# A graph layer on one core: the TensorE fetch moves to three bf16 parts of its table and takes 24 chunks over five late chunks each, in place of 20 over seven

## The reference, cut to what matters

```python
xs = x[src]                                              # 200000 edges, x is 6250 x 64, float32
deg_w = max(seg(w), 1);  deg_c = max(seg(1), 1)          # seg sums over the edges with the same dst
gcn   = seg((w / sqrt(deg_w[src] * deg_w[dst]))[:, None] * xs) @ Wgcn + bgcn
sage  = x @ Wsage_s + seg(xs) / deg_c[:, None] @ Wsage_n + bsage
agg_w = seg(w[:, None] * xs)
gin   = ((1 + gin_eps) * x + agg_w) @ Wgin + bgin
gconv = x @ Wgc1 + agg_w @ Wgc2 + bgc
eop   = seg(w[:, None] * relu(xs + edge_attr)) @ Wedge + bedge
out   = layernorm(x + sum_k weights[k] * [gcn, sage, gin, gconv, eop][k])
```

## Time and profile before

| | us |
|---|---|
| median of three runs | 2227.15 (2219.24 to 2228.43) |
| the profiled execution's own time | 2228.75 |
| its span, first to last instruction | 2226.9 |
| first late product of the rounds, to the first of the plain step | 475.70 to 2166.97 |
| last late product starts | 2189.03 |
| indirect DMAs on POOL for late chunks | 1280 |
| mean granted TensorE clock | 0.867 |

### The profile page before, as it was taken

How to read it: one execution, slowest core, us unless ns; L and a number is a source line. 1 busy time by engine, 2 the same in 40 slices (tenths; PEclk the granted TensorE clock), 3 DMA queues, 4 the chain that set the end, 5 groups by cost and what they waited for, 6 DMA issues and landing times.

```text
span 2226.9 us, 22565 instructions
## 1 busy us (share of the span) xinstructions
PE 1556.4 (70%) x6037; PEld 1007.5 (45%) x6037; DVE 928.6 (42%) x2539; ACT 826.9 (37%) x1201; POOL 1355.2 (61%) x1426
## 2 busy tenths in 40 slices
PE   1004367566888777877878778777887888877876
PEld 1003367553554544544445445444444445544546
DVE  5684256543433332433433433243333334423346
ACT  1676233243433433424244234233333324423323
POOL 7665366556666656656666666566666656665660
PEclk9999967688989888978889888888888888888988
DMA  5111234331222222222222222222222222222223
GB/s 98 23 24 51 70 100 112 95 80 42 51 64 45 55 54 46 57 46 44 54 57 53 47 57 43 47 58 50 48 66 43 48 51 57 47 53 44 59 55 77
DMA packets 83186, 126.12 MB, mean 57 GB/s; under 512 B 29494, under 2 KB 31269, under 8 KB 82821
## 3 DMA queue, kind: packets, MB, share of 16 engines
q0 software_dynamic: 45056, 48.85, 13.6%
q1 hardware_dynamic: 36371, 74.90, 11.0%
q10 hardware_dynamic: 1650, 1.04, 0.2%
HBM read 121.29 MB, written 3.40 MB: 56 GB/s over the span
## 4 chain that ended last, share of the span: by engine, by line
PE 43%; issue 18%; another core or an unknown queue 17%; DVE 10%; ACT 4%; POOL 3%; DVEq 2%; DMA 1%; SPq 0%; POOLq 0%; ACTq 0%
PE psum L1280 27%; PE psum L1261 13%; ACT ring L604 4%; POOL ring L559 3%; DVE ring L1076 2%; DVE sums L1065 2%; DVE early L988 1%; PE psum L1312 1%; PE psum L1228 1%; DVE attr L953 1%; DVE early L992 1%; DMA ring<-node_table,idx 1%; PE psum L1341 1%; PE psum L1342 1%
## 5 line engine op out<-in xcount | busy, mean ns | idle before, releaser
L559 POOL DMA_INDIRECT ring<-node_table,idx x1280 | 1228.4, 960 | 758.2 <-issue 389.4
L1280 PE MATMUL psum<-table_sb,early_x 128*128 128x455 f32 x2240 | 988.1, 586 | 115.6 <-issue 110.1
L1280 PEld LDWEIGHTS psum<-table_sb,early_x 128*128 128x128 f32 x2240 | 446.0, 205 | 573.4 <-issue 566.7
L1261 PE MATMUL psum<-ring 128*128 128x120 f32 x2560 | 405.3, 313 | 246.5 <-issue 127.5
L1261 PEld LDWEIGHTS psum<-ring 128*128 128x128 f32 x2560 | 375.5, 224 | 310.2 <-issue 164.9
L988 DVE TENSOR_TENSOR early<-psum,digit_hot 128x455 f32<-128x455 f32 x160 | 100.6, 631 | 989.5 <-remote 599.3
L688 ACT ACTIVATE early_x<-early,minus_ids 128x256 f32<-128x256 f16 x560 | 370.4, 744 | 138.7 <-remote 103.4
L655 ACT ACTIVATE ring<-attr 128x512 f32<-128x512 f32 x160 | 100.2, 626 | 483.4 <-DVE attr L953 383.8
L679 ACT ACTIVATE early<-early 128x256 f32<-128x256 f32 x40 | 16.7, 416 | 518.2 <-DVE early L1009 385.1
L1065 DVE TENSOR_TENSOR sums<-sums,psum 64x40 f32 (+1 forms) x648 | 127.5, 197 | 97.4 <-remote 53.6
L526 POOL DMA_INDIRECT early_x<-in_x,early_idx x128 | 122.0, 953 | 61.4 <-issue 40.3
(11 more groups left out here) (158 smaller groups left out, 644.8 us busy)
## 6 DMA issues: line engine op xcount, KB each, us to landing
attr<-in_edge_attr SPq DMA_DIRECT2D x79, 512.0 KB
ring<-node_table,idx POOLq DMA_INDIRECT x1280
early<-in_edge_attr SPq DMA_DIRECT2D x36, 256.0 KB
src_all<-in_src SPq DMA_DIRECT2D x16, 512.0 KB
early<-key_rows SPq DMA_DIRECT2D x10, 512.0 KB
early_x<-degree_rows SPq DMA_DIRECT2D x2, 1568.0 KB
early_x<-in_x,early_idx POOLq DMA_INDIRECT x128
node_table<-table_sb SPq DMA_DIRECT2D x1, 1666.0 KB, 6.0
```

Source lines behind the costliest of these rows:

```text
L559: nc.gpsimd.indirect_dma_start(out=feat[:, u, j, D:BLOCK], out_offset=None, in_=table, in_offset=bass.IndirectOffsetOnAxis(ap=idx[:, u, j: ...
L1261: last = nc.tensor.matmul(to[:, 0:3 * WINDOW], features[:, j, 0:2 * D], hots[:, j].rearrange("p k n -> p (k n)"), start=(j == 0), stop=(j ...
L1280: last = nc.tensor.matmul(pick_ps[k % 2].rearrange("p (b c) -> p b c", b=SPLIT), node_hot[:, k, a], table_sb[:, a * SPLIT:(a + 1) * SPLIT, ...
```

## The change

The picked chunks grow from 20 to 24, so the late ones fall from 160 to 156. A picked chunk is spread over five late chunks in place of seven: PE has two tiles in slots 0, 2 and 4 and one in slots 1 and 3; ACT makes its blocks in slots 0, 1, 2 and 4; the first unit's features and relu come in slot 3, its product in slot 4. Six rounds of 4 x 5 slots follow the early steps (five of them in the loop), and then PLAIN = 5 steps, 20 late chunks, stand alone.

The tile's product changes its operands. The table is cut into three bf16 parts that add up to it exactly: the upper halves of its words (`x_high`), the upper halves of the rest (`x_mid`), and what then remains (`x_low`). The first two are read with a step of two bf16 out of float32 words, the last is packed. The one-hot becomes bf16 too. A tile is then 7 x 3 = 21 bf16 matmuls, not 7 float32 ones. DVE makes the rest and the low part in the last early step (`split_table`), in four pieces, one for each of its chunks.

```diff
-PICKED = 20
+PICKED = 24
-SLOTS = 7
+SLOTS = 5
-PLAIN = 1
+PLAIN = 5
...
-        HOT = SPLIT * P
-        at_hots = HEAD * TILES * D
+        COLS = D + 1
+        at_rest = HEAD * TILES * D
+        at_low = at_rest + NT * COLS
+        at_hots = at_low + -(-NT * COLS // 2)
+        HOT = SPLIT * P // 2
-        node_hot = early_flat[:, at_hots:at_hots + HALF * HOT].rearrange(
+        node_hot = early_flat[:, at_hots:at_hots + HALF * HOT].bitcast(BF16).rearrange(
             "p (k a e) -> p k a e", k=HALF, a=SPLIT)
+        def upper_halves(t):
+            return t.bitcast(BF16).rearrange("p (t c two) -> p t c two", t=NT, two=2)[:, :, 0:COLS, 1]
+        x_rest_flat = early_flat[:, at_rest:at_low]
+        x_rest = x_rest_flat.rearrange("p (t c) -> p t c", c=COLS)
+        x_high = upper_halves(table_sb[:, :, :].rearrange("p t c -> p (t c)"))
+        x_mid = upper_halves(x_rest_flat)
+        x_low = early_flat[:, at_low:at_hots].bitcast(BF16)[:, 0:NT * COLS].rearrange("p (t c) -> p t c", c=COLS)
+        PIECES = UNROLL
+        pieces = [slice(k * 2 * SPLIT, min((k + 1) * 2 * SPLIT, NT)) for k in range(PIECES)]
...
-            return (((0, 0),), ((0, 1),), ((0, 2),), ((0, 3),), ((1, 0),), ((1, 1),), ((1, 2), (1, 3)))[r]
+            return (((0, 0), (0, 1)), ((0, 2),), ((0, 3), (1, 0)), ((1, 1),), ((1, 2), (1, 3)))[r]
-        HOT_BLOCKS = {0: (0, 0), 2: (0, 1), 4: (1, 0), 6: (1, 1)}
+        HOT_BLOCKS = {0: (0, 0), 1: (0, 1), 2: (1, 0), 4: (1, 1)}
...
-                        if r == 4:
+                        if r == 3:
                             relu_unit(2 * c, 0)
...
+                def split_table(k):
+                    tiles = pieces[k]
+                    nc.vector.tensor_tensor(out=x_rest[:, tiles], in0=table_sb[:, tiles, 0:COLS], in1=x_high[:, tiles],
+                                            op=ALU.subtract).then_inc(rest_ready, 1)
+                    dve.wait_ge(rest_ready, v * PIECES + k + 1)
+                    nc.vector.tensor_tensor(out=x_low[:, tiles], in0=x_rest[:, tiles], in1=x_mid[:, tiles],
+                                            op=ALU.subtract).then_inc(low_ready, 1)
...
                             early_features(c)
+                        if splitting:
+                            split_table(u)
...
-                            if r == 4:
+                            if r == 3:
                                 unit_features(2 * c, c, 0)
...
+                    pe.wait_ge(low_ready, (v + 1) * PIECES)
+                    parts = (x_high, x_mid, x_low)
                     for a in range(SPLIT):
-                        last = nc.tensor.matmul(pick_ps[k % 2].rearrange("p (b c) -> p b c", b=SPLIT), node_hot[:, k, a],
-                                                table_sb[:, a * SPLIT:(a + 1) * SPLIT, 0:D + 1],
-                                                start=a == 0, stop=a == SPLIT - 1)
+                        for n_part, part in enumerate(parts):
+                            last = nc.tensor.matmul(pick_ps[k % 2].rearrange("p (b c) -> p b c", b=SPLIT), node_hot[:, k, a],
+                                                    part[:, a * SPLIT:(a + 1) * SPLIT],
+                                                    start=(a, n_part) == (0, 0), stop=(a, n_part) == (SPLIT - 1, len(parts) - 1))
...
-                        if r == 5:
+                        if r == 4:
                             unit_product(2 * c, 0)
```

More of the change, by code:

```diff
@@ L193, in build @@
         digit_hot = sb("digit_hot", [P, PICKED * TILES, SPLIT], BF16)
-        HOT = SPLIT * P
-        at_hots = HEAD * TILES * D
-        assert at_hots + HALF * HOT <= EARLY * TILES * D
-        node_hot = early_flat[:, at_hots:at_hots + HALF * HOT].rearrange(
-            "p (k a e) -> p k a e", k=HALF, a=SPLIT)
+        COLS = D + 1
[3 more added lines that the diff above has]
+        HOT = SPLIT * P // 2
+        assert at_hots + HALF * HOT <= EARLY * TILES * D and at_hots <= (EARLY - UNROLL + 1) * TILES * D and at_low <= (EARLY - UNROLL) * TILES * D
+        node_hot = early_flat[:, at_hots:at_hots + HALF * HOT].bitcast(BF16).rearrange(
+            "p (k a e) -> p k a e", k=HALF, a=SPLIT)
+        def upper_halves(t):
[7 more added lines that the diff above has]
+        pieces = [slice(k * 2 * SPLIT, min((k + 1) * 2 * SPLIT, NT)) for k in range(PIECES)]
+        assert pieces[-1].stop == NT
         root_src = sb("root_src", [P, TILES])
@@ L316, in build @@
         key_bias_set, key_row_step = sem("key_bias_set"), sem("key_row_step")
+        rest_ready, low_ready = sem("rest_ready"), sem("low_ready")
         node_far, node_hot_made, picked = sem("node_far"), sem("node_hot_made"), sem("picked")
@@ L961, in weigh_hots, with early_step @@
                     weigh(hot[:, u], 2, wroot[:, u]).then_inc(hots_ready, 1)
-                def early_step(i, begun=True, chunks=UNROLL):
+                def split_table(k):
[5 more added lines that the diff above has]
+                                            op=ALU.subtract).then_inc(low_ready, 1)
+                def early_step(i, begun=True, chunks=UNROLL, splitting=False):
                     firsts = first_windows(dve, BASE - LAG + i * UNROLL, UNROLL)
@@ L1114, in _ @@
                     early_step(i)
-                early_step(EARLY_STEPS - 1)
+                early_step(EARLY_STEPS - 1, splitting=True)
                 turn(0, begun=False)
```

## The result

The changed kernel took 2429.09 us (median of 4 runs, 2403.31 to 2433.54) against 2227.79 us for the kernel before beside it (4 runs). Over these and two further runs of the changed kernel (2414.89 and 2419.92 us) the ratio is 1.0865, 95% interval 1.0794 to 1.0936: it is 8.7% slower. The forecast was 2250 us, range 2165 to 2320.

A forecast was written before the change was run, and what follows sets the result against it. The rounds were taken as bound by POOL and PE leaning on each other. 475.7 + 4 + 24 x 63.5 + 200.6 + 10 = 2214.3 us to the last product, +21.5 over before, gave 2250 us, range 2165 to 2320.

The forecast's parts named there:

- The bf16 pass: In PE's tile fetch, a bf16 pass of 455 columns takes 0.191 us, so a tile of 21 passes 4.01 us.
- the rival of slow passes: In PE's tile fetch, a bf16 pass lasts as long as a float32 one: tile 8.02 us, total 2994 us; chance 0.05.
- The split: Cutting the table on DVE in the last early step adds 4 us to the path, bounds 0 and 12.5.
- the plain stretch and the tail: After the rounds, 17 remaining chunks at 11.8 us take 200.6 us, and the end behind the last gather 10 us.
- the rival of the free plain stretch: In the 20 late chunks alone POOL's pauses vanish, 31 us less: 2219 us, no change; chance 0.03.
- The new wait of slot 3: PE waits 3.8 us once a picked chunk for ACT's relu, behind the unit's relu and the block.
- the old losses in proportion to late chunks, 27.5 x 5/7 = 19.6: In the rounds, PE's losses per picked chunk shrink from 27.5 to 19.6 us with five late chunks for seven.
- a POOL that is held up stretches their issue less: In the rounds, late consumers delay POOL, which eases PE's slow issue; period taken as 63.5 us, under the upper 66.2.
- POOL's waits for ACT's copy more often than 18 times: Sign expected in the trace: POOL waits for ACT's copy more often than the earlier 18 times.
- the forecast's case: In the rounds, a picked chunk's period lies from 61.5 to 65.5 us, total 2202 to 2298 us; chance 0.43.
- The floor of 59.0 us: In the rounds, POOL alone sets the period at 5 x 11.8 = 59.0 us, total 2142 us; rival's chance 0.28.
- Nothing is given back: In the rounds, the period stays at its upper bound of 66.2 us, total 2315 us; rival's chance 0.21.

The follow-up runs named there:

- indices_first: The changed kernel with ACT's copy of the next gather indices one slot earlier: 1817.8 us, 0.9916 of the kernel before on the same fast chip.
- both moves: The changed kernel with ACT's index copy one slot earlier and the unit's relu one slot later: 2211.4 and 2215.4 us, 0.9904 and 0.9876 of before.
- bf16_old_order_3: The kernel before with only its fetch changed to three bf16 parts, on a slow chip: 2258.4 us, 1.0163 of before.
- bf16_old_order: The kernel before with only its fetch changed to three bf16 parts, on a fast chip: 1834.0 us, 1.0016 of before.

## Why the prediction was wrong, by its own steps

**The bf16 pass.** Forecast 0.191 us. In the timeline of PE three passes recur in 0.605 us (granted clock 0.96 from 1169 to 1177):

```profile
1169.94 0.37 PE L1311 MATMUL psum<-table_sb,early_x 128*128 128x455 bf16 x1
...
1176.59 0.37 PE L1311 MATMUL psum<-table_sb,early_x 128*128 128x455 bf16 x1
```

6.65/33 = 0.2015 us, so a tile is 4.23 us, not 4.01, and a picked chunk's work 44.5, not 42.8. This explains 1.7 of the 7.4 us. The stepped operands cost nothing that shows, and the rival of slow passes fell. The estimate of 192 ns by the formula of the Trainium skill (page TensorE: Matmul & The Clock Gate, section Back-to-back issue gap) lies 10 ns under this row; the 131 ns that the section gives for a sustained stream of 512 columns is not seen here.

**The split, the plain stretch and the tail.** The split shows nowhere (the early steps took 199 us, 207 before). The plain stretch is 11 us shorter than forecast: there GpSimd ran up to five chunks without a pause, at 10.0 us, and paused 3.90, 7.09 and 7.67 us at 2205, 2262 and 2319. Of the 31 us that the rival of the free plain stretch named, 11 came true.

**The new wait of slot 3.** Forecast 3.8 us before the late product of slot 4. Measured there: 3.4 to 3.7 us in every picked chunk of indices_first (kind B), and 91.1/24 = 3.8 us in the changed kernel's first profile (kind A). Mechanism right, size right. What the forecast left out is that TensorE's old wait for DVE's masks goes in exchange: all its waits for DVE and ACT together are 136.6/24 = 5.7 us a picked chunk, against 110.1/20 = 5.5 before.

**The period: the step that failed.** It is the sentence "the old losses in proportion to late chunks, 27.5 x 5/7 = 19.6", with what follows it: that late consumers hold GpSimd up and "a POOL that is held up stretches their issue less". On kind A the losses, new wait included, are 70.9 - 44.5 = 26.4 us a picked chunk, against 27.5 before and at most 23.4 forecast. The 7.4 us between 63.5 and 70.9 are 1.7 for the longer pass, 3.0 for losses over 23.4, and 2.7 that the forecast took as given back and that did not come. By kinds of loss, TensorE's "issue" went from 12.6 to 11.5 us a picked chunk where 5/7 of it is 9.0. Its busy time over the work at full clock went from 67.0 - 57.1 = 9.9 to 54.1 - 44.5 = 9.6 where 5/7 is 7.1. The waits for DVE and ACT stayed 2.0 under the sum's terms.

Two things stood against the proportion. First, the late copy. Being held up for 13 us did not relieve TensorE: it gave GpSimd 16 gathers to issue in one run, and TensorE's issue slowed at the run's end, and with it the signal of a finished tile, for which the pick, the unit, the block and so the next copy wait. The prediction named the sign of it ("POOL's waits for ACT's copy more often than 18 times", 38 in all, 34 in the rounds) and followed ScalarE's queue in slot 3 to the next relu, but not to the copy of indices that stands between block and relu at every second late chunk. It gave that copy no price; the runs give 192 us. Second, the number of passes: long runs of gathers did fall about as forecast, from 55/20 = 2.8 to 42/24 = 1.8 a picked chunk, but each goes with 6.6 us of "issue" in place of 4.6, and the bf16 fetch alone raised that figure from 4.8 to 9.8. With the copy moved the period is 63.8 us, with both moves 62.4: the forecast's case (61.5 to 65.5), for a kernel that wasn't the one changed. That it lands there is partly luck, since the price of a long run was wrong in it too.

**The rivals.** The floor of 59.0 us was reached by no variant on kind A. It was never GpSimd's own: its 11.8 us hold pauses of 3.4 to 3.7 us, in which GpSimd waited for TensorE's product where the rows name a releaser. "Nothing is given back", 66.2, pointed the right way, and its reason, that slow issue strikes instructions, is what bf16_old_order_3 shows in direction; it fell short by 4.7 us, 3.0 of losses and 1.7 of the longer pass.

## What to carry to other kernels

When an in-order engine gets a wait moved up in its queue, price everything behind it up to the next item of every other engine, the small copy that feeds a DMA queue first: 0.19 us of work in the wrong place cost 192 us here. A loss that looks proportional to the work may belong to a rhythm; before scaling it, ask what sets the rhythm after the change. And three short passes for two long ones shorten a kernel only where nothing else sets its pace and the engine gets its instructions fast enough: in the old order they earned nothing where GpSimd set the pace (kind B), and cost 1.6% where TensorE's idle "issue" time grew by more than the passes saved (kind A).

## What the runs showed of the hardware

The same kernel before took 1826 to 1835 us in every run on three chips and 2215 to 2256 us in every run on three others. The gathers themselves are no slower: a gather's mean is 959 ns in bf16_old_order on kind B and 964 ns on kind A. What differs is the time between instructions. One group of PE's fetch passes in that kernel, kind B and then kind A (count, busy us, mean ns, idle before and its releasers):

```profile
L1311 PE MATMUL psum<-early_x 128*128 128x455 bf16 x2240 | 654.1, 374 | 0.0
```

```profile
L1311 PE MATMUL psum<-early_x 128*128 128x455 bf16 x2240 | 719.3, 398 | 195.1 <-issue 192.7 <-ACT ring L672 1.4
```

and GpSimd's waits on kind A, where kind B has only its 0.3 us between gathers:

```profile
POOL ring L576 <- remote: 260.6, 89, 5.0
POOL ring L576 <- ACT idx L670: 92.9, 10, 31.5
```

The signals differ too. In the traces of kind B the semaphore of a tile is raised within 0.02 us of the modelled end of its last pass, for each of the 192 tiles of indices_first; in the changed kernel on kind A 98 of 192 come over 1 us late, the latest by 21.8 us. GpSimd's own pace without a pause, 1.25 us a gather, is the same on both.

So the stretched issue of the earlier trace rows and the pauses of the earlier trace rows, on which the forecast's 11.8 us a chunk and 27.5 us of losses rest, belong to the chips of kind A. On kind B TensorE has at most some 12 us of "issue" in the rounds of any run, against 156 to 486 on kind A, and GpSimd has no wait marked "remote" there. Why these chips issue and signal more slowly behind a long run of gathers no run tells. For the change it decides what can be gained: with the unit's relu moved, the new order with the bf16 fetch is 2.0% faster than before on kind B, where four picked chunks more are 32 gathers less; with both moves it is 1.0 to 1.2% faster on kind A, the best version found there. Whether that is the merit of the change is open: no run put the two moves into the order of before, where GpSimd waits 75.3 us for the copy as well. Whether the changed kernel as it is would be slower on kind B was not seen; with its index copy moved it is 0.8% faster there.
